# x multiplied by W1 ahead of the products of A, and 24 products of the last three rows made from fp32r halves

## The chip, the cores and the metric

The kernel runs on one core of a Trainium2 chip. The metric is the device time of one execution in microseconds (us); lower is better.

## What is computed

One layer over N = 8192 nodes with D = 128 features. `adj` is a dense 8192 x 8192 matrix of 268 MB, so reading it once is a large part of the time.

```
def _lap_mul(A, x):
    d = 1.0 / jnp.sqrt(jnp.sum(A, axis=-1))
    return d[:, None] * (A @ (d[:, None] * x))
z = _lap_mul(A, x) @ W1 + b1
z = jax.nn.leaky_relu(z, negative_slope=0.1)
sq = jnp.sum(z * z, axis=-1)
d2 = jnp.maximum(sq[:, None] + sq[None, :] - 2.0 * (z @ z.T), 0.0)
S = jnp.exp(-jnp.sqrt(d2 + 1e-10) / 2.0)
S = the 4 largest of each row of S, the rest zero
out = _lap_mul(S + A, x) @ W2 + b2
return _layernorm(x + out)
```

## The kernel before

A is cut into 16 x 16 tiles ("quads") of 512 rows by 512 columns. Tile (b, q) is row block b, column block q, and it arrives by one DMA of 1 MB into one of 18 slots in SBUF as 128 x 2048 numbers. Engines: PE is TensorE, DVE is VectorE, ACT is ScalarE, POOL is GpSimd, and SP issues the loads. Each engine runs its own list in the written order and waits on semaphores.

**Stage 1, rows 0 to 15.** For each row b, SP loads the 16 tiles of the row. DVE adds them one after the other into a running `total` (`add_quad`, line 1481), folds the total twice (`add_tiles`, 1486 and 1487), PE sums it over partitions (`row_sums`, 776), DVE copies the sums (`read_sums`, 1491), ACT takes the root (1046), DVE makes d by one Newton step (432 to 440) and scales x of that row by it (`scale_xs`, 1499). In between, PE multiplies tiles with those parts of the scaled x that already exist (`product`, 767): four fp32 matmuls of 128 x 512 for each tile. 158 of the 256 products are made in stage 1. A row's sum in PSUM is saved by ACT to R2 (1057) once its last product is made. A slot is loaded again after its tile was added and multiplied. At the end of row 15 the scaled x is split in two fp32r parts, a rounded one (ACT, 1031) and the rest (DVE, 1505).

**Stage 2.** The other 98 tiles are loaded again and multiplied from halves: ACT rounds the tile to fp32r (`round_2`, 1039), DVE subtracts to get the rest (`rest_2`, 1564), and PE makes eight matmuls with the rounded half (830 and 831) and four with the rest (834). Two buffers hold rounded halves, so the rounding of tile n waits for the product of tile n - 2. The rows of A come in the order 0, 15, 14, 1, 2, ..., 13. When a row is complete, its z is made beside the products of the next row: DVE adds the two parts of y (`make_y`, 1537), PE multiplies by W1 (`z_raw`, 796), DVE applies d, b1 and the leaky step (`make_z`, 1547 and 1550), PE transposes z back (`z_transposed`, 806), ACT squares (1070) and splits it (1076, 1079), DVE makes the rest (`make_zl`, 1556) and PE sums the squares (`squares`, 813). The table `made` says after which product each step stands.

**Stage 3 and later.** PE forms z z^T in pieces of 1024 columns (866 to 874), ACT copies them (1141), and DVE finds the largest of each row (1621, 1624), while A is read a third time for the last product, there with POOL making the rests (1299, 1442). The change leaves this part as it was, but for the steps at its start.

The order of the work is written out by hand, with counts at which a step is placed. Which slot a load goes to is worked out by `next_slot`, which takes the slot that comes free first.

Of the kernel before, what the change touches and what calls it, by code (L numbers as in the profile page):

```python
# [27 lines left out]
SLOTS_END = (0, 1, 2, 3, SLOTS_2, SLOTS_2 + B // TB)  # L28
# [7 lines left out]
LOW_AT = 10  # L36
ROW_BANKS = (2, 0, 3)
# [91 lines left out]
def build(nc, x, at, W1, b1, W2, b2, consts, out, xs_dram, xh_dram, xl_dram, acc_dram):  # L129
# [31 lines left out]
    for n in range(n_one + len(two)):  # L161
        if n < n_one - STREAM_END:
            k = next_slot(n, [*range(SLOTS_A), *(k for k, b in SLOTS_Y.items() if left(n) <= B * (b + 1)),
# [9 lines left out]
        now[k] = n  # L173
    last_in = {}
# [3 lines left out]
    with ctx:  # L178
# [25 lines left out]
        b1r = sb("b1r", [P, D])  # L204
# [19 lines left out]
        total = R1[:, N + 2 * SLOT:N + 3 * SLOT]  # L224
# [4 lines left out]
        y = tmp[:, 0:BC]  # L229
        zn = tmp[:, BC:2 * BC].rearrange("p (j d) -> p j d", j=TB)  # L230
        window = tmp[:, 2 * BC:2 * BC + WIN]
        junk = tmp[:, 2 * BC + 256:2 * BC + 256 + P]
# [34 lines left out]

        acc_x2 = sb("acc_x2", [P, len(ROWS_X) - 1, BC], at=top_of["xgl"])
# [6 lines left out]
        al_2 = [sb(f"al_2{k}", [P, TB, BC], F32R, at=top_of["R1"] + k * SLOT * 4) for k in range(2)]  # L275
        x_last = sb("x_last", [P, 2, 2, TB, D], F32R, at=over1 + 2 * SLOT * 4)
# [7 lines left out]
        spare = R2[:, (B - 1) * BC:B * BC]  # L284
        raw_t = [R1[:, k * SLOT:(k + 1) * SLOT].rearrange("p (k c) -> p k c", c=BC) for k in range(3)]
# [52 lines left out]
        xl_ok = sem("xl_ok")  # L338
        rnd_2 = sem("rnd_2")
        al_ok = sem("al_ok")  # L340
        y_ok = sem("y_ok")
        zraw = sem("zraw")
        zn_ok = sem("zn_ok")
        sq_ok = sem("sq_ok")
        zt = sem("zt")
# [99 lines left out]
        halves = range(min(q for r, q in two), B)  # L445
# [16 lines left out]
        for n, (b, q) in enumerate(two):  # L462
            last_quad[b] = n + 1
        CHAIN = 9
# [181 lines left out]
        def _(sp):  # L646
# [6 lines left out]
            sp.dma_start(b1r[:, :], b1.partition_broadcast(P)).then_inc(s_const, 16)  # L653
            sp.dma_start(b2r[:, :], b2.partition_broadcast(P)).then_inc(s_const, 16)
            for n, (b, q) in enumerate(one + two):
# [11 lines left out]
                if n < n_one and n % B == B // 2:  # L667
# [4 lines left out]
                    sp.dma_start(xs[:, tiles], x[:, tiles]).then_inc(s_x[n // B], 16)  # L672
# [81 lines left out]
        def _(pe):  # L754
# [3 lines left out]
            def product(b, q):  # L758
# [5 lines left out]
                if first and b >= YB:  # L764
                    pe.wait_ge(y_saved, b - YB + 1)
                for k in range(TB):
                    i = pe.matmul(PS[:, b % YB], xs[:, q * TB + k], slots_a[slot_of[n]][:, k],  # L767
                                  start=first and k == 0, stop=prod_at[b, q] == closed[b] and k == TB - 1)
                i.then_inc(prod1, 1)

            def row_sums(b):
                pe.wait_ge(part_ok, b + 1)
                if b >= 1:
                    pe.wait_ge(sums_read, b)
# [4 lines left out]
            for b in range(B):  # L779
                sums_at = len(products[b]) - (SUMS_EARLY if b == B - 1 else 0)  # L780
                for r, q in products[b][:sums_at]:
# [8 lines left out]
            def z_raw(pi):  # L790
                b = blocks2[pi]
                pe.wait_ge(y_ok, pi + 1)
                if pi >= 1:
                    pe.wait_ge(zn_ok, pi)
                for j in range(TB):
                    i = pe.matmul(PS[:, 4, j * P:(j + 1) * P], y[:, j * P:(j + 1) * P], w1[:, :],
                                  start=True, stop=True)
                i.then_inc(zraw, 1)

            def z_transposed(pi):  # L800
                pe.wait_ge(zn_ok, pi + 1)
                if pi >= 1:
                    pe.wait_ge(zl_ok, pi)
                    pe.wait_ge(z2_ok, pi)
                for j in range(TB):
                    i = pe.transpose(PS[:, 5, j * P:(j + 1) * P], zn[:, j], ident[:, :])
                i.then_inc(zt, 1)
# [11 lines left out]
            assert made[B - 2] == len(two) - 1  # L819
            for n, (b, q) in enumerate(two):  # L820
# [6 lines left out]
                pe.wait_ge(xl_ok, q - halves[0] + 1)  # L827
# [9 lines left out]
                for pi in range(B):  # L837
                    if n == made[pi] + 6:
                        squares(pi)
                    if n == made[pi] + 3:  # L840
                        z_transposed(pi)
                    if n == made[pi]:
                        z_raw(pi)


            def scores(g, j, c, first):
# [3 lines left out]
                if first and j == 0:  # L850
                    pe.wait_ge(z2_ok, min(B, 2 * c + 4))
# [73 lines left out]
            def group_pe(g, odd):  # L925
                for j in range(GT):
                    for c in range(NE):
                        scores(g, j, c, is_first(g))
                        if is_first(g) and (j, c) == (0, 0):
                            z_raw(B - 1)  # L930
                            z_transposed(B - 2)
                            squares(B - 3)
                        if is_first(g) and (j, c) == (0, 1):
                            z_transposed(B - 1)
                            squares(B - 2)
                        if is_first(g) and (j, c) == (0, 2):
                            squares(B - 1)
                        if is_first(g) and (j, c) == (PLAIN_TILES - 1, NE - 1):
# [834 lines left out]
```

## Time and profile before

| | us |
|---|---|
| median of 3 runs | 2691.74 (2691.24 to 2696.32) |
| span of the profiled execution, first to last instruction | 2759.5 |
| stage 1, to the end of its last product | 719.8 |
| stage 2, from there to the end of its last product | 306.4 |
| first score tile complete and everything after | the rest |

The profiled execution shows no time of its own beside its span; the first instruction stands 0.3 us after its start. The stages are read from the chain of work that ended last, whose rows carry start and duration.

### The profile page before, as it was taken

How to read it: one execution, taken by the hardware profiler on the slowest of the kernel's cores; microseconds unless marked ns; L12 is line 12 of the kernel's file. 1: busy time of each engine (PE TensorE's matmuls, PEld its weight loads, DVE VectorE, ACT ScalarE, POOL GpSimd, SP SyncE). 2: the span in 40 equal slices, each digit the busy share in tenths (PEclk: the TensorE clock that was granted, in tenths of full speed). 3: DMA queues.
4: the chain of work that ended last, by engine and by line, in shares of the span. 5: the costliest groups of instructions: out<-in, count | busy, mean ns of one | idle time of the engine just before them, and what ended most of it. 6: DMA issues, size and time to landing. Idle time of an engine off the chain costs nothing.

```text
span 2759.5 us, 29107 instructions
## 1 busy us (share of the span) xinstructions
PE 2482.6 (90%) x9356; PEld 1722.4 (62%) x9356; DVE 2319.8 (84%) x1411; ACT 1606.7 (58%) x1905; POOL 1195.4 (43%) x987
## 2 busy tenths in 40 slices
PE   1367999999999998899999999999999987888978
PEld 0133444444677776578787877778787764666655
DVE  7998899977788888999999999999999773666766
ACT  0000000000477767999989899899988763555655
POOL 0000000000000000377778878788878956666760
PEclk9688999999999999999999999999999988999989
DMA  9999999995899960146555655555655688988975
GB/s 385 421 402 408 398 421 421 421 421 215 320 349 342 338 226 7 35 141 183 151 163 138 179 142 175 140 170 149 174 143 167 182 309 343 347 324 320 345 295 208
DMA packets 147949, 718.58 MB, mean 260 GB/s; under 512 B 19025, under 2 KB 26961, under 8 KB 86609
## 3 DMA queue, kind: packets, MB, share of 16 engines
q1 hardware_dynamic: 124384, 670.49, 65.6%
q0 software_dynamic: 18800, 37.77, 5.7%
q10 hardware_dynamic: 4608, 8.39, 0.8%
q8 instruction: 79, 1.29, 0.2%
q14 instruction: 78, 0.63, 0.1%
HBM read 680.40 MB, written 36.18 MB: 260 GB/s over the span
## 4 chain that ended last, share of the span: by engine, by line
PE 56%; issue 10%; ACT 10%; DVE 9%; DMA 7%; POOL 3%; another core or an unknown queue 3%; SPq 0%; ACTq 0%; POOLq 0%; DVEq 0%
PE PS L767 17%; PE PS L866 5%; PE PS L868 5%; PE PS L867 5%; DMA ring<-at 4%; ACT R L1141 3%; PE PS L834 3%; PE PS L910 3%; PE PS L921 3%; PE PS L911 3%; PE PS L830 2%; PE PS L831 2%; ACT ah_t L1191 2%; DVE R L1621 2%
## 5 line engine op out<-in xcount | busy, mean ns | idle before, releaser
L1299 POOL TENSOR_TENSOR al<-ring,ah 128x1024 fp32r<-128x1024 f32 x264 | 644.0, 2441 | 180.5 <-ACT ah L1112 168.7
L1621 DVE MAX8 R<-R 128x8 f32<-128x8192 f32 x64 | 555.9, 8685 | 68.1 <-ACT R L1141 67.9
L1141 ACT ACTIVATE R<-PS 128x1024 f32<-128x1024 f32 x512 | 518.1, 1018 | 114.1 <-PE PS L874 83.1
L1624 DVE FIND_INDEX8 R<-R,R 128x8 uint32<-128x8192 f32 x64 | 555.9, 8685 | 0.3 <-issue 0.3
L1272 POOL CAST zst<-zh 128x128 fp32r<-128x128 f32 (+1 forms) x64 | 26.2, 410 | 1113.2 <-DVE zl L1556 811.5
L866 PE MATMUL PS<-zh,zst 128*128 128x512 f32 x1024 | 407.3, 398 | 28.6 <-ACT PS L1127 12.7
L868 PE MATMUL PS<-zh,zst 128*128 128x512 f32 x1024 | 400.4, 391 | 0.0
L867 PE MATMUL PS<-zl,zst 128*128 128x512 f32 x1024 | 400.1, 391 | 0.0
L1456 POOL DMA_INDIRECT R<-xs_dram,R x256 | 279.7, 1093 | 145.2 <-issue 75.5
L1127 ACT ACTIVATE PS<-R 128x1024 f32<-128x1024 f32 x310 | 318.0, 1026 | 6.6
L1046 ACT ACTIVATE tiny<-rowsum 128x4 f32<-128x4 f32 x16 | 3.3, 205 | 481.2 <-DVE rowsum L1491 481.2
L767 PE MATMUL PS<-cache,R 128*128 128x512 f32 x584 | 262.9, 602 | 17.0 <-DMA cache<-at 11.6
L1481 DVE TENSOR_TENSOR R<-R,cache 128x2048 f32<-128x2048 f32 x106 | 242.9, 2292 | 21.2 <-DMA cache<-at 19.0
L866 PEld LDWEIGHTS PS<-zh,zst 128*128 128x128 f32 x1024 | 192.1, 188 | 97.0 <-ACT PS L1127 25.3
L981 PE MATMUL PS<-ah_t,xsh 128*128 128x512 f32 x368 | 162.9, 443 | 63.9 <-ACT ah_t L1191 45.0
L868 PEld LDWEIGHTS PS<-zh,zst 128*128 128x128 f32 x1024 | 192.2, 188 | 41.7
L867 PEld LDWEIGHTS PS<-zl,zst 128*128 128x128 f32 x1024 | 192.3, 188 | 39.8 <-issue 0.7
L767 PEld LDWEIGHTS PS<-cache,R 128*128 128x128 f32 x584 | 112.1, 193 | 157.6 <-issue 144.1
L767 PE MATMUL PS<-ring,R 128*128 128x512 f32 x384 | 177.4, 610 | 11.2 <-DMA ring<-at 5.7
L1564 DVE TENSOR_TENSOR al<-ring,ah 128x2048 fp32r<-128x2048 f32 x66 | 151.0, 2290 | 35.6 <-ACT ah L1039 33.1
L1481 DVE TENSOR_TENSOR R<-R,ring 128x2048 f32<-128x2048 f32 x72 | 165.0, 2292 | 11.5 <-DMA ring<-at 9.6
L1668 DVE TENSOR_TENSOR al_t<-R,ah_t 128x1024 fp32r<-128x1024 f32 x98 | 115.7, 1221 | 63.2 <-ACT ah_t L1191 36.9
(177 smaller groups left out, 4469.9 us busy)
## 6 DMA issues: line engine op xcount, KB each, us to landing
R<-at SPq DMA_DIRECT2D x152, 1024.0 KB, 13.3
ring<-at SPq DMA_DIRECT2D x148, 1024.0 KB, 9.5
ring<-at SPq DMA_DIRECT2D x264, 512.0 KB, 3.9
cache<-at SPq DMA_DIRECT2D x117, 1024.0 KB, 20.2
raw_sq<-at SPq DMA_DIRECT2D x21, 1024.0 KB
raw_z<-at SPq DMA_DIRECT2D x20, 1024.0 KB
raw_ring<-at SPq DMA_DIRECT2D x20, 1024.0 KB
acc_dram<-R POOLq DMA_DIRECT2D x78, 256.0 KB, 5.7
```

The costliest lines, as they stand in the source:

```text
L767: i = pe.matmul(PS[:, b % YB], xs[:, q * TB + k], slots_a[slot_of[n]][:, k], start=first and k == 0, stop=prod_at[b, q] == closed[b] and k ...
L866: pe.matmul(bank, zst[:, par, 0], zh[:, cols], start=not on_seed, stop=False, skip_group_check=True)
L867: pe.matmul(bank, zst[:, par, 0], zl[:, cols], start=False, stop=False, skip_group_check=True)
L868: i = pe.matmul(bank, zst[:, par, 1], zh[:, cols], start=False, stop=on_seed, skip_group_check=True)
L981: pe.matmul(bank, xsh[:, t], ah_t[n % 2][:, k], start=from_zero and k == 0, stop=False, skip_group_check=True)
L1127: act.activation(pair(False, 0, c), sq_row[c], ACT.Copy).then_inc(seeded, 1)
L1141: act.activation(score[j % 2][:, c * EC:(c + 1) * EC].rearrange("p (b c) -> p b c", b=2), pair(first, j, c), ACT.Copy).then_inc(copied, 1)
L1299: pool.tensor_tensor(al[:, k % SPLIT], raw[k % RAW], ah[:, k % SPLIT].bitcast(F32), ALU.subtract)\
L1456: pool.indirect_dma_start(gx[f % 2][:, j, m], None, xs_dram, bass.IndirectOffsetOnAxis(ap=sidx[:, FIN[f] * TB + j, m:m + 1], axis=0))\
L1481: v.tensor_tensor(total.rearrange("p (k c) -> p k c", c=BC), other, slots_a[slot_of[n]], ALU.add)\
L1621: v.max(top[:, j], score[j % 2]).then_inc(dve3, 1)
L1624: v.max_index(place[:, j], top[:, j], score[j % 2]).then_inc(placed, 1)
```

## The change

W1 is moved ahead of A: since (A (d x)) W1 = A (d (x W1)), PE multiplies each x block by W1 in stage 1 (`x_w1`, from a transposed copy of x, `xt`, that is loaded in place of x), and ACT copies the product over x (`xw_ok`) before DVE scales it. In stage 2 the multiplication by W1 and the transposes of z are gone. In their place d lies along the free axis: PE transposes it once (`turn_d`), ACT writes it to DRAM, and ACT's queue loads it again for each row, spread over all partitions (`load_d`), so that DVE multiplies y by it; ACT adds b1 (`add_b1`). The squares come from one small transpose for each half of the rows (`turn_squares`, `read_squares`) in place of ACT's accumulating squares.

In rows 13, 14 and 15, the 8 products of each row with column blocks 0 to 7 are made from halves as in stage 2: ACT rounds the tile (`round_1`), POOL subtracts and writes the rest over the tile (`low_1`), PE makes 8 + 4 fp32r matmuls (`product_of_halves`). The halves of x for these blocks are made in row 12 (`high_of_low_q` on ACT, four subtractions on POOL). The order of the products of these rows is mixed (`mixed`). From row 12 on the running total lies in PSUM, and four of the slots are no longer loaded.

```
-STREAM_END = 12
+STREAM_END = 5
+LATE, TOTAL_AT, QL = 13, 12, 8
+W1_EARLY = 3
...
+            def x_w1(b):
+                pe.wait_ge(s_x[b], 16)
                 if b >= 1:
                     pe.wait_ge(sums_read, b)
                 for j in range(TB):
+                    i = pe.matmul(PS[:, YB, j * P:(j + 1) * P], xs[:, b * TB + j], w1[:, :], start=True, stop=True)
+                i.then_inc(xw, 1)
+
+            def product_of_halves(b, q, first):
+                m = half_1[b, q]
+                low = low_1[slot_of[load_at[b, q]]]
+                pe.wait_ge(xl_low_q, 4)
+                pe.wait_ge(rnd_1, m + 1)
+                for k in range(TB):
+                    t = q * TB + k
+                    pe.matmul(PS[:, y_bank(b)], xsh[:, t], ah_2[m % 2][:, k], start=first and k == 0, stop=False)
+                    pe.matmul(PS[:, y_bank(b)], xl_q[:, t], ah_2[m % 2][:, k], start=False, stop=False)
+                pe.wait_ge(al_1, m + 1)
+                for k in range(TB):
+                    i = pe.matmul(PS[:, y_bank(b)], xsh[:, q * TB + k], low[:, k], start=False, stop=False)
+                i.then_inc(prod1, 1)
...
-            def z_raw(pi):
...
-            def z_transposed(pi):
...
+            def round_1(m):
+                n = load_at[halved_1[m]]
+                act.wait_ge(ld_a[slot_of[n]], turn_of[n])
+                if m < 2:
+                    free_of_stage_1(act, SLOTS_B + m)
+                else:
+                    act.wait_ge(prod1, prod_at[halved_1[m - 2]])
+                act.activation(ah_2[m % 2][:, :, :], slots_a[slot_of[n]], ACT.Copy).then_inc(rnd_1, 1)
...
+            def add_b1(pi):
+                act.wait_ge(y_ok, pi + 1)
...
+                act.activation(z[pi % 2], y[pi % 2], ACT.Identity, bias=b1c[:, 0:1]).then_inc(biased, 1)
+                if pi + 2 < B:
+                    load_d(pi + 2)
...
+            for m, bq in enumerate(halved_1):
+                n = load_at[bq]
+                raw_1 = slots_a[slot_of[n]]
+                pool.wait_ge(rnd_1, m + 1)
+                pool.wait_ge(rows_added, (B - 1) * (n // B) + max(n % B, 1))
+                pool.tensor_tensor(low_1[slot_of[n]][:, :, :], raw_1, ah_2[m % 2][:, :, :].bitcast(F32), ALU.subtract)\
+                    .then_inc(al_1, 1)
...
+                running = PS[:, 3:3 + TB] if b >= TOTAL_AT else total
+                other = slots_a[slot_of[n - 1]] if i == 1 else running
+                v.tensor_tensor(total if i == B - 1 else running, other, slots_a[slot_of[n]], ALU.add)\
...
                     v.wait_ge(prod2, last_quad[b])
-                    v.tensor_tensor(y, cols, PS[:, bank_2[b]], ALU.add).then_inc(y_ok, 1)
+                    link(v.tensor_tensor(y[pi % 2], cols, PS[:, bank_2[b]], ALU.add))
+                    cols = y[pi % 2]
+                v.wait_ge(s_d_all[pi % 2], 16 * (pi // 2 + 1))
+                v.tensor_tensor(y[pi % 2], cols, d_all[:, pi % 2], ALU.mult).then_inc(y_ok, 1)
```

PE at the turn from row 12 to row 13. Before, the sums of row 12 (L776) stand among products that are all fp32 (cache, ring, R_49 and R_50 on the left of the comma are slots of tiles; a count stands for matmuls of 128 x 512):

```order
L767 MATMUL PS<-R_50,R_49 128x512 x4
L767 MATMUL PS<-cache,R_49 128x512 x12
L776 MATMUL PS<-ones,R_49 128x1 x4
L767 MATMUL PS<-ring,R_49 128x512 x4
L767 MATMUL PS<-R_49 128x512 x4
L767 MATMUL PS<-cache,R_49 128x512 x20
```

In the changed kernel the same place has x W1 of row 12 (L835) three products ahead of the sums (L856), and after two whole products the first one from halves (rounded halves ah, rests low; the pair L845, L846 stands four times):

```order
L835 MATMUL PS<-w_58,R_49 128x128 x4
L826 MATMUL PS<-cache,R_49 128x512 x8
L826 MATMUL PS<-ring,R_49 128x512 x4
L856 MATMUL PS<-ones,R_49 128x1 x4
L826 MATMUL PS<-cache,R_49 128x512 x4
L826 MATMUL PS<-ring,R_49 128x512 x4
L845 MATMUL PS<-ah_83,xsh 128x512
L846 MATMUL PS<-ah_83,xl_q 128x512
...
L849 MATMUL PS<-low_90,xsh 128x512 x4
```

Four 128 x 128 matmuls came in ahead of each row's sums, and a halved product now stands where a whole one did.

DVE in stage 2, from the eighth y of the stage on (al is the rest of a tile). Before:

```order
L1537 TENSOR_TENSOR R_49<-R_50,PS 128x512
L1564 TENSOR_TENSOR al_83<-R_49,ah_81 128x2048
L1564 TENSOR_TENSOR al_84<-R_49,ah_82 128x2048
L1547 SCALAR_TENSOR_TENSOR R_49<-PS,dsc,b1r 128x128 x4
L1550 SCALAR_TENSOR_TENSOR R_49<-R_49 128x512
L1564 TENSOR_TENSOR al_83<-ring,ah_81 128x2048
```

and the same place in the changed kernel:

```order
L1701 TENSOR_TENSOR R_49<-R_50,PS 128x512
L1704 TENSOR_TENSOR R_49<-R_49,d_all 128x512
L1723 TENSOR_TENSOR al_85<-R_49,ah_83 128x2048
L1723 TENSOR_TENSOR al_86<-R_49,ah_84 128x2048
L1708 SCALAR_TENSOR_TENSOR R_49<-R_49 128x512
```

The four small steps are gone from the second gap between rests, and a second step of 512 columns has come into the first one.

ACT in stage 2, beside the steps of one row's z (ah is the rounded half). Before:

```order
L1039 ACTIVATE ah_82<-ring 128x2048
L1070 ACTIVATE R_49,sq<-R_49 128x128 x4
L1039 ACTIVATE ah_81<-R_49 128x2048
L1076 ACTIVATE zh<-PS 128x512
L1079 ACTIVATE R_49<-PS 128x512
```

And in the changed kernel:

```order
L1118 ACTIVATE ah_83<-R_49 128x2048
L1212 ACTIVATE yz_odd<-yz_odd,b1c 128x512
L1205 DMA d_all<-d_dram 128x512
L1118 ACTIVATE ah_84<-R_49 128x2048
L1118 ACTIVATE ah_83<-ring 128x2048
L1219 ACTIVATE zh<-yz_odd 128x512
L1222 ACTIVATE R_49<-yz_odd 128x512
```

The four squares are replaced by one step of 512 columns and a DMA that ACT issues.

## Rows read from the trace of the kernel before

**Rows 1.** The head of the page.

```profile
span 2759.5 us, 29107 instructions
```

**Rows 2.** Chain that ended last, stages 1 and 2: start, duration, what.

```profile
268.30 40.42 PE PS L767 x88
...
607.60 51.61 PE PS L767 x120
...
709.39 10.41 PE PS L767 x24
...
1024.94 1.21 PE PS L834 x4
```

**Rows 3.** Timeline of PE at the sums of row 14: start, duration, instructions.

```profile
659.04 0.95 PE L776 MATMUL PS<-ones,R 128*128 128x1 f32 x8
659.85 3.68 PE L767 MATMUL PS<-cache,R 128*128 128x512 f32 x8
```

**Rows 4.** Timeline of PE in rows 4 to 6; idle time before, and its releaser.

```profile
218.83 1.87 PE L776 MATMUL PS<-ones,R 128*128 128x1 f32 x8 [5.50 <-DVE R L1487]
...
268.30 6.09 PE L767 MATMUL PS<-ring,R 128*128 128x512 f32 x8 [3.81 <-DMA ring<-at]
```

**Rows 5.** Busy time by stretch: length, engines' busy us, clock, DMA share, GB/s.

```profile
621.00:690.00 69.00, 69.00 (x169) 30.97 (x168) 48.83 (x31) 6.07 (x12) 0.00 (x0) 1.00 0.57 216
```

**Rows 6.** Groups of instructions, later stages: count, busy us, mean ns, idle before.

```profile
L1442 POOL TENSOR_TENSOR al_t<-R,ah_t 128x2048 fp32r<-128x2048 f32 x2 | 9.1, 4558 | 0.5 <-ACT ah_t L1191 0.5
L1299 POOL TENSOR_TENSOR al<-ring,ah 128x1024 fp32r<-128x1024 f32 x264 | 644.0, 2441 | 180.5 <-ACT ah L1112 168.7 <-PE PS L921 1.6 <-POOL d2s L1354 0.6
...
L1624 DVE FIND_INDEX8 R<-R,R 128x8 uint32<-128x8192 f32 x64 | 555.9, 8685 | 0.3 <-issue 0.3
```

**Rows 7.** Groups of instructions up to 1100 us.

```profile
L1481 DVE TENSOR_TENSOR R<-R,cache 128x2048 f32<-128x2048 f32 x106 | 242.9, 2292 | 21.2 <-DMA cache<-at 19.0
...
L1057 ACT ACTIVATE R<-PS 128x512 f32<-128x512 f32 x16 | 9.1, 596 | 215.1 <-PE PS L767 215.1
```

**Rows 8.** Timeline of PE over one row of stage 2.

```profile
843.46 0.39 PE L830 MATMUL PS<-ah,xsh 128*128 128x512 f32 x1
...
846.18 0.39 PE L830 MATMUL PS<-ah,xsh 128*128 128x512 f32 x1
...
849.05 1.05 PE L796 MATMUL PS<-w,R 128*128 128x128 f32 x8
849.86 0.47 PE L830 MATMUL PS<-ah,xsh 128*128 128x512 f32 x1
...
851.79 1.08 PE L834 MATMUL PS<-al,xsh 128*128 128x512 f32 x4
...
858.60 0.60 PE L806 MATMUL PS<-ident,R 128*128 128x128 f32 x4
858.95 0.48 PE L830 MATMUL PS<-ah,xsh 128*128 128x512 f32 x1
...
867.40 1.02 PE L813 MATMUL PS<-R 128*128 128x512 f32 x2
867.85 0.79 PE L830 MATMUL PS<-ah,xsh 128*128 128x512 f32 x1
...
873.74 1.05 PE L796 MATMUL PS<-w,R 128*128 128x128 f32 x8
```

**Rows 9.** Timeline of DVE over the same row of stage 2.

```profile
851.25 2.29 DVE L1564 TENSOR_TENSOR al<-R,ah 128x2048 fp32r<-128x2048 f32 x1 [0.49 <-ACT ah L1039]
...
854.62 0.69 DVE L1550 SCALAR_TENSOR_TENSOR R<-R 128x512 f32<-128x512 f32 x1
```

**Rows 10.** Timeline of ACT over the same row of stage 2.

```profile
852.96 1.92 ACT L1039 ACTIVATE ah<-ring 128x2048 fp32r<-128x2048 f32 x1 [1.74 <-PE PS L834]
```

**Rows 11.** Timeline of PE at the sixth and seventh score piece.

```profile
1042.18 0.39 PE L866 MATMUL PS<-zh,zst 128*128 128x512 f32 x1
...
1043.99 0.39 PE L866 MATMUL PS<-zh,zst 128*128 128x512 f32 x1
```

More of the change, by code:

```diff
@@ L83, in held, with mixed, y_bank, row_of_y_bank @@
     return range(b - DEFER[b], b)
+def mixed(b):
+    plain, halved = list(range(QL, b)), list(range(QL))
+    order = [plain.pop(0), plain.pop(0)]
+    n_plain, n_halved, taken = len(plain), len(halved), 0
+    while plain or halved:
+        if halved and (QL - len(halved) + 1) * n_plain <= (taken + 1) * n_halved or not plain:
+            order.append(halved.pop(0))
+        else:
+            order.append(plain.pop(0))
+            taken += 1
+    return order
+def y_bank(b):
+    return b % YB if b < 9 else (b + 2) % 3
+def row_of_y_bank(b):
+    return b - YB if b < 12 and b != 10 and b != 11 else b - 3
 def plan_ab():
@@ L173, in build @@
         now[k] = n
+    order_1 = []
+    for b in range(B):
+        sums_at = len(products[b]) - (SUMS_EARLY if b == B - 1 else 0)
+        order_1 += [(b, q) for b, q in products[b][:sums_at]] + [("sums", b)] + products[b][sums_at:]
+    order_1 += products[B]
+    place_1 = {what: n for n, what in enumerate(order_1)}
+    halved_1 = [(b, q) for b, q in flat if b >= LATE and q < QL]
+    half_1 = {bq: m for m, bq in enumerate(halved_1)}
+    last_whole = max(prod_at[bq] for bq in flat if bq[1] < QL and bq not in half_1)
     last_in = {}
@@ L444, in build @@
         ends = list(itertools.accumulate(sum(r == b for r, q in two) for b in blocks2))
-        halves = range(min(q for r, q in two), B)
+        halves = range(QL, B)
         last_quad = {}
@@ new lines, in after @@
+            def after(k):
+                return place_1[one[last_in[k]]] + 0.5
+            steps = []
+            for b in range(TOTAL_AT, B):
+                steps.append((place_1["sums", b] + 0.7, "root", b))
+            for b in range(saved, B):
+                steps.append((place_1[flat[closed[b] - 1]] + 0.6, "save", b))
+            for k in range(2):
+                steps.append((after(SLOTS_2 + k), "high", k))
+            steps.append((after(SLOTS_2 + B // TB + 1), "move", 0))
+            for q in halves[:-2]:
+                steps.append((max(after(SLOTS_2 + k // TB) for k in range(QL, q + 1)) + 2.2 + q / 100, "half", q))
@@ new lines, in _ @@
+            for m in range(len(halved_1)):
+                at_m = place_1[halved_1[m - 2]] + 0.5 if m >= 2 else place_1[halved_1[m]] - 3.5
+                steps.append((at_m, "round", m))
+            for _, what, k in sorted(steps):
+                if what == "root":
+                    b = k
+                    act.wait_ge(xw, b + 1)
+                    act.activation(xs[:, b * TB:(b + 1) * TB], PS[:, YB].rearrange("p (j d) -> p j d", j=TB), ACT.Copy)\
+                       .then_inc(xw_ok, 1)
+                    root_of_row(b)
+                    if b == B - 1:
+                        round_2(0)
+                        for q in halves[-2:]:
+                            high_half(q)
+                        round_2(1)
+                if what == "save":
+                    save_y(k)
+                if what == "high":
+                    high_of_low_q(k)
+                if what == "move":
+                    move_low()
+                if what == "half":
+                    high_half(k)
+                if what == "round":
+                    round_1(k)
```

267 lines of the change are left out of this document (157 added, 110 removed).

## The prediction

> **What bounds the kernel now.** I read the page first for the span [rows 1], then the chain that ended last, then PE's timeline where the chain is PE, and last the timelines of DVE and ACT in stage 2. The profiled execution spans 2759.5 us; the median of the runs is 2691.74, 67.8 lower. I make the sum in the profiled execution's microseconds and take the difference over to the median as it is: the stretches that change are PE's own work, one matmul behind the other, and no row tells which stretch the 67.8 lie in.
>
> The chain shows that from 268.30 on stage 1 is PE alone: 40 to 52 us of line 767 at a time, broken only by the row sums, to 719.8 [rows 2]. 120 records are 15 products, so a product costs 51.61 / 15 = 3.44 us; the sums cost 0.81 (659.04 to 659.85) [rows 3]. Up to 268 PE waits for others: 5.50 us for DVE's total at row 4's sums, 3.81 for a load at row 6's first product [rows 4]. In the last rows the DMA is only 57% busy while PE is busy throughout [rows 5], so PE time saved there needs no faster loads.
>
> Stage 2 (719.8 to 1026.15, 306.4 us) is also a dense PE, but a tight one. A product from halves takes 2.72 (843.46 to 846.18) [rows 8]. Round 2 of tile n starts only after product n - 2: ACT 1.92, DVE 2.29, and the rest must be there when PE has done the first two thirds of product n. With about 0.26 from product to ACT (the start at 852.96 [rows 10]; the four matmuls from 851.79 take 0.91 [rows 8]) and 0.1 for the two handovers, that is 0.26 + 1.92 + 2.29 + 0.1 = 4.57, against 2.72 + 1.81 = 4.53 on PE. So anything put between two rests on DVE that is longer than its gap (0.49 before the rest at 851.25 [rows 9]) is a wait on PE.
>
> **The change part by part.**
>
> *x W1 in stage 1 costs 8.7.* The same four matmuls as z_raw: 849.05 to 849.86 and 0.08 on the first record after (0.47 against 0.39), 0.89 [rows 8]; the row sums, also eight records, cost 0.81. I take 0.87. In rows 0 to 5 PE waits for longer than that [rows 4], so it is hidden; if that cover fails it is 5 more. In rows 6 to 15 it is on the path: 10 x 0.87 = 8.7. ACT's copy of it has three products (10 us) to finish 0.6 us of work [rows 7].
>
> *24 products from halves give 17.2.* 24 x (3.44 - 2.72).
>
> *Their supply takes back 5.* POOL's subtraction of 128 x 2048 is 4.56 us [rows 6], twice DVE's. 24 of them are 109 us, and PE spends about 147 us on these three rows (row 13: 8 x 2.72 + 6 x 3.44 + 1.7 = 44), so POOL keeps up on average. Locally it doesn't: with two buffers, product m can't end before product m - 2 plus 0.26 + 1.92 + 4.56 + 0.05 + 0.91 = 7.7, where two halved products in a row need 5.44. A third in a row waits 2.3. The order has three in a row twice, both in row 13: (13,2) to (13,4), and (13,5) to (13,7), where the queue on POOL is partly made up by then: 2.3 + 1.4. Pairs wait 0.2 to 0.6, five of them: 1.3. Bounds: 0, were the rounds early enough, and 17, where nothing is gained.
>
> *DVE and POOL in the same rows: 7, unknown.* POOL's first subtraction of a row starts when DVE has added that tile, the third load of the row; DVE then does the Newton steps and scale_xs from SBUF and after them the add that frees POOL's next subtraction. If these DVE steps had to wait while POOL reads SBUF, each of rows 13 and 14 loses 4.56 less 0.5 of slack on its second halved product; row 15, with a whole product between, 1.5; and add_tiles of row 15 comes up to two subtractions late, of which 3.4 reach PE. Sum 13. The other end is 0: in the later stages DVE's FIND_INDEX8, listed with two inputs from SBUF, takes 8685 ns beside POOL's 2441 [rows 6], both undisturbed. But its second input is eight values, so that row doesn't decide; I take the middle, 7. The Trainium skill ("SBUF — State Buffer", Who interferes with whom) says that a DVE instruction with two SBUF inputs and a GpSimd one that reads SBUF exclude each other for a whole instruction; by it this term is 13 and the sum 6 worse. No row before has such a pair. With the total in PSUM the 14 later adds of a row have one SBUF input and stay clear of it.
>
> *Loads.* From row 12 on there are four slots less. A load then goes into a slot whose product is about 10 places (30 us) back, against 4.9 us for 1 MB at the 216 GB/s of these rows [rows 5]: 0. The last load waits for (15,4), leaving three products (8.9) for the load (4.9), its add (2.29) and a fold of about 2: 0.3, inside the 5.
>
> *Stage 2 gives 12.* Gone for each row: z_raw 0.89 and the transposes 0.43 (0.35 and 0.08) [rows 8], 15 and 14 times before the end: 19.4. Squares stay at 0.86. One row of 8 products now takes 24.69 (849.05 to 873.74): 21.76 + 0.89 + 0.43 + 0.86 leave 0.75 of waits. In the changed order DVE has the add and the multiplication by d in one gap: 0.6 + 0.04 + 0.6 (a 128 x 512 step counts 0.69 [rows 9], of which I take 0.6 for one in a stream), 1.24 less 0.43 is 0.8 of wait; add_b1 waits for it and delays the next rounding, another 0.3. So 1.1 a row against 0.75. By these prices the 98 products, 14 squares and 1.1 x 14 make 266.6 + 12 + 15.4 = 294, 12.4 less than 306.4. Bounds: no waits, -27; twice the waits, +3. turn_d, turn_squares, the copy of d and ACT's wait for the write of d at the fifth product: 1 to 4 us once; 2.
>
> *The start of the scores gives 2.5.* Before, the sixth piece starts at 1042.18 [rows 11], 16.0 after stage 2. A piece takes 1.81 (1042.18 to 1043.99). After: five pieces (9.1), three squares of 0.86 (2.6), and by estimate 1.8 for turn_squares, a first wait and the copy of the squares: 13.5. ACT's squares and PE's two transposes were on that path. Bounds 0 and -4.
>
> Sum: 8.7 - 17.2 + 5 + 7 - 12.4 + 2 - 2.5 = -9.4. Later stages stay. **Forecast 2682.3 us.**
>
> **The rivals.**
>
> *No exclusion between DVE and POOL* (0 in place of 7): -16.4, 2675. For it: nothing in the trace shows the two disturb each other. Against: no such pair stands in it.
>
> *Full exclusion* (the rule above): -3.4, 2688. Its sign would be lost in the measurement, 0.2% or 5.4 us.
>
> *POOL sets the pace, and the kernel is slower.* 4.56 is from two instructions beside other DVE work. At more than 5.2 us most subtractions (some 17 of 24) end after PE wants them, and each further 0.1 us costs 1.7. With the -9.4 it decides from about 5.6; at 6.0 it gives +11, 2703. Against: 264 subtractions of half the size agree at 2441.
>
> *Stage 2 gives nothing.* DVE's step is late because d lands late (each load_d of 256 KB runs beside a DMA near its full rate) or the waits are 2 us a row: the 12.4 go, +3, 2695. Against: load_d is issued two rows ahead, 14 us or more.
>
> **How the numbers follow.** Chances: forecast (that term between 3 and 10) 0.40, no exclusion 0.18, full exclusion 0.20, POOL paced 0.12, stage 2 nothing 0.10. The forecast's own range is 2676 to 2688. For 8 in 10 the range must take in full and no exclusion with the bounds of stage 2's waits, and part of the slower cases: 2669 to 2699. Faster: 0.36 of the forecast's 0.40, the 0.18 and 0.06 of full exclusion, 0.60. Slower: the 0.12 and 0.03 of the last, 0.15. Same: 0.25.
>
> **What would show it.** In rows 6 to 12 the sums should lie 0.87 further apart. In rows 13 to 15 the whole products stay at 3.44 and halved ones stand at 2.72 with waits for POOL near (13,4) and (13,7); if DVE's short Newton steps stand some 4 us apart there, exclusion is real. A subtraction on POOL over 5 us speaks for the third rival. Stage 2 should last 296 and its row of 8 products 23.7 to 23.8, with PE waiting for the rest once after each y. The sixth score piece should start about 13.5 after the last product. I am wrong if stage 1 ends later than 727 or stage 2 lasts over 302.

## The result

The changed kernel takes 2703.07 us (median of 6 runs, 2698.41 to 2704.70), the kernel before 2692.23 (6 runs); the ratio is 1.0032, 95% interval 1.0022 to 1.0043. It is 10.8 us or 0.3% slower, where 9.4 us less were forecast, and the time lies outside the forecast's range of 2669 to 2699.

The head of the changed kernel's page, then PE's timeline at some row sums (L856), at the last product of stage 1 (L826) and at the last one of stage 2 (L913): start, duration, what, and in brackets the idle time before and its releaser.

```profile
span 2701.3 us, 29187 instructions
```

```profile
350.19 0.95 PE L856 MATMUL PS<-ones,R 128*128 128x1 f32 x8
...
393.17 0.95 PE L856 MATMUL PS<-ones,R 128*128 128x1 f32 x8
...
561.68 0.95 PE L856 MATMUL PS<-ones,R 128*128 128x1 f32 x8
...
724.81 1.85 PE L856 MATMUL PS<-ones,R 128*128 128x1 f32 x8 [3.26 <-DVE R L1655]
...
735.18 3.60 PE L826 MATMUL PS<-ring,R 128*128 128x512 f32 x8
...
1036.79 1.19 PE L913 MATMUL PS<-al,x_last 128*128 128x512 f32 x4
```

DVE's timeline at the first search for the largest scores:

```profile
1059.28 8.68 DVE L1792 MAX8 R<-R 128x8 f32<-128x8192 f32 x1
```

The same two places in the kernel before, the sums of row 12 (PE) and the first search (DVE):

```profile
557.69 0.95 PE L776 MATMUL PS<-ones,R 128*128 128x1 f32 x8
```

```profile
1048.99 8.70 DVE L1621 MAX8 R<-R 128x8 f32<-128x8192 f32 x1 [7.56 <-ACT R L1141]
```

Before, the sums of row 12 stood at 557.69, stage 1 ended at 719.8, stage 2 at 1026.15 [rows 2], and the first MAX8 at 1048.99. Now they are at 561.68, 738.6 (735.18 + 3.44), 1038.0 and 1059.28. So up to row 12 the change costs 4.0; rows 13 to 15 take 176.9 where they took 162.1, +14.8; stage 2 takes 299.4 where it took 306.4, -7.0; the start of the scores takes 21.3 where it took 22.8, -1.5. That is +10.3 at the first MAX8, which is the whole loss within the spread of the runs.

The loss is made in rows 13 to 15. PE's timeline at four halved products and the products behind them (L849 are the matmuls with the rest, L826 whole products):

```profile
577.90 1.93 PE L849 MATMUL PS<-low,xsh 128*128 128x512 f32 x4 [3.72 <-POOL low L1429]
579.64 4.52 PE L826 MATMUL PS<-cache,R 128*128 128x512 f32 x8
...
597.06 1.20 PE L849 MATMUL PS<-low,xsh 128*128 128x512 f32 x4 [2.19 <-POOL low L1429]
598.09 5.29 PE L826 MATMUL PS<-ring,R 128*128 128x512 f32 x8
...
614.25 1.20 PE L849 MATMUL PS<-low,xsh 128*128 128x512 f32 x4 [2.67 <-POOL low L1429]
615.29 5.29 PE L826 MATMUL PS<-cache,R 128*128 128x512 f32 x8
...
636.62 2.07 PE L849 MATMUL PS<-low,xsh 128*128 128x512 f32 x4 [3.72 <-POOL low L1429]
```

Each time PE waits for the rest, and the whole product behind the wait takes 4.1 to 5.3 (4.11 behind the last, at 638.50) in place of 3.60 as listed. The group of these matmuls up to 1060 us (busy, mean ns, idle before) shows the sum of such waits, 14.4:

```profile
L849 PE MATMUL PS<-low,xsh 128*128 128x512 f32 x96 | 29.0, 427 | 14.4 <-POOL low L1429 14.4
```

Why the rest is late stands in the timelines of POOL (first fence) and DVE (second) at the start of row 13:

```profile
565.19 4.51 POOL L1429 TENSOR_TENSOR low<-ring,ah 128x2048 fp32r<-128x2048 f32 x1 [7.17 <-DVE PS L1649]
573.32 13.71 POOL L1429 TENSOR_TENSOR low<-cache,ah 128x2048 fp32r<-128x2048 f32 x3 [3.61 <-DVE PS L1649]
```

```profile
565.16 0.16 DVE L487 TENSOR_TENSOR tiny<-tiny 128x4 f32<-128x4 f32 x1
565.36 4.37 DVE L488 TENSOR_TENSOR tiny<-tiny,rowsum 128x4 f32<-128x4 f32 x1
569.87 0.17 DVE L490 TENSOR_SCALAR tiny<-tiny 128x4 f32<-128x4 f32 x1
...
719.06 4.97 DVE L1654 TENSOR_TENSOR R<-R 128x1024 f32<-128x1024 f32 x1
```

A Newton step on 128 x 4 numbers takes 4.37 and ends at 569.73, when POOL's subtraction ends (569.70). The add that POOL's second subtraction needs stands behind it on DVE, so POOL idles 3.61 and PE waits 3.72. The same repeats in row 14 (624.09). At the end of row 15 the fold (L1654, 1.2 to 1.4 in the rows before) takes 4.97 beside a subtraction, and PE waits 3.26 before the last sums.

What the waits leave behind is in the busy times by stretch (length, PE, PEld, DVE, ACT, POOL, granted clock, DMA share, GB/s):

```profile
572.00:580.00 8.00, 4.28 (x15) 3.17 (x14) 7.90 (x4) 1.98 (x2) 6.55 (x2) 0.88 0.66 266
580.00:598.00 18.00, 15.81 (x52) 9.71 (x51) 17.73 (x9) 6.28 (x4) 12.60 (x4) 0.96 0.69 263
598.00:603.00 5.00, 5.00 (x11) 2.16 (x9) 4.90 (x4) 1.91 (x1) 5.00 (x2) 0.66 0.83 318
...
615.00:621.00 6.00, 6.00 (x16) 2.89 (x16) 0.00 (x0) 2.39 (x2) 0.00 (x0) 0.72 1.01 427
621.00:638.50 17.50, 13.78 (x45) 8.41 (x45) 16.71 (x12) 2.12 (x2) 10.83 (x3) 0.93 0.73 263
638.50:661.00 22.50, 21.92 (x73) 13.67 (x72) 22.16 (x11) 8.25 (x5) 17.38 (x5) 0.98 0.75 296
...
718.00:726.50 8.50, 5.24 (x22) 3.95 (x21) 8.43 (x7) 3.00 (x6) 4.95 (x2) 0.90 0.69 247
726.50:732.00 5.50, 5.50 (x14) 4.32 (x15) 4.37 (x13) 3.05 (x4) 0.00 (x0) 0.53 0.00 0
```

From 598 to 603 PE is busy throughout at a mean of 0.66 of the full clock, for at least 2 us of it, 599 to 601, at 0.50, the lower of its two levels (1.2 of 2.4 GHz); before this it had waited 2.19. Length times missing share over these eight rows is 10.2 us, a little of it idle. In the kernel before, the clock was 1.00 in the stretch of these rows that is shown [rows 5], and it is 1.00 over all of them (557.69 to 719.80).

Stage 2: DVE (first fence) and PE (second) around one y.

```profile
864.54 0.68 DVE L1701 TENSOR_TENSOR yz_odd<-R,PS 128x512 f32<-128x512 f32 x1
865.25 0.69 DVE L1704 TENSOR_TENSOR yz_odd<-yz_odd,d_all 128x512 f32<-128x512 f32 x1
865.86 2.28 DVE L1723 TENSOR_TENSOR al<-R,ah 128x2048 fp32r<-128x2048 f32 x1
```

```profile
868.20 1.19 PE L913 MATMUL PS<-al,xsh 128*128 128x512 f32 x4 [0.52 <-DVE al L1723]
...
892.23 1.20 PE L913 MATMUL PS<-al,xsh 128*128 128x512 f32 x4 [0.45 <-DVE al L1723]
```

A row of eight products is 24.03 long (868.20 to 892.23), where it was 24.69 [rows 8].

### The profile page after: what moved, and what is told of

Read it like the earlier page. It is cut to its first block, busy times and chain, and to the rows that moved or that the text cites. A ratio compares the mean times of both kernels' runs of the same rounds, so it can differ in the third digit from the quotient of the medians.

```text
span 2701.3 us, 29187 instructions
## 1 busy us (share of the span) xinstructions
PE 2459.1 (91%) x9405; PEld 1729.9 (64%) x9405; DVE 2346.9 (87%) x1363; ACT 1655.7 (61%) x1835; POOL 1320.0 (49%) x1015
## 4 chain that ended last, share of the span: by engine, by line
PE 51%; ACT 14%; DVE 11%; issue 11%; DMA 9%; POOL 4%; SPq 0%; ACTq 0%; POOLq 0%; DVEq 0%
PE PS L826 14%; ACT R L1293 6%; DMA ring<-at 5%; PE PS L945 4%; PE PS L947 4%; PE PS L946 4%; PE PS L1049 3%; PE PS L989 2%; PE PS L1000 2%; PE PS L990 2%; PE PS L913 2%; ACT PS L1278 2%; DMA raw_sq<-at 2%; DVE R L1792 2%; DVE al_t L1839 2%
## 5 line engine op out<-in xcount | busy, mean ns | idle before, releaser
L945 PE MATMUL PS<-zh,zst 128*128 128x512 f32 x1024 | 408.4, 399 | 29.4 <-ACT PS L1278 12.4
L1422 POOL TENSOR_TENSOR xl_q<-R,xsh 128x1024 fp32r<-128x1024 f32 x4 | 10.7, 2708 | 546.9 <-PE PS L826 546.9
L826 PE MATMUL PS<-cache,R 128*128 128x512 f32 x496 | 225.0, 604 | 5.7 <-DVE R L1667 5.7
L1649 DVE TENSOR_TENSOR R<-R,cache 128x2048 f32<-128x2048 f32 x78 | 178.8, 2292 | 13.8 <-DMA cache<-at 12.4
L1059 PE MATMUL PS<-ah_t,xsh 128*128 128x512 f32 x368 | 155.4, 422 | 19.1 <-ACT ah_t L1342 19.0
L826 PEld LDWEIGHTS PS<-cache,R 128*128 128x128 f32 x496 | 95.6, 195 | 118.8 <-issue 117.7
L826 PE MATMUL PS<-ring,R 128*128 128x512 f32 x336 | 157.0, 614 | 7.9 <-DVE R L1667 5.4
L1263 ACT ACTIVATE ah<-ring 128x1024 fp32r<-128x1024 f32 x152 | 159.8, 1051 | 4.1 <-DMA ring<-at 4.1
L1118 ACT ACTIVATE ah<-ring 128x2048 fp32r<-128x2048 f32 x66 | 126.4, 1915 | 46.4 <-PE PS L913 43.5
```

Source lines behind the costliest of these rows:

```text
L826: i = pe.matmul(PS[:, y_bank(b)], xs[:, q * TB + k], slots_a[slot_of[n]][:, k], start=first and k == 0, stop=prod_at[b, q] == closed[b] an ...
L945: pe.matmul(bank, zst[:, par, 0], zh[:, cols], start=not on_seed, stop=False, skip_group_check=True)
L1263: act.activation(ah[:, k % SPLIT], raw[k % RAW], ACT.Copy).then_inc(rounded, 1)
L1649: v.tensor_tensor(total if i == B - 1 else running, other, slots_a[slot_of[n]], ALU.add)\
```

## The experiments

Rows 13 to 15 are counted from the sums of row 12 to the end of the last product of stage 1, since the loads shift the place of these sums by up to 4 us from run to run. Each kernel and the kernel before were timed on one chip, and the ratio is between these two; the chips differ from kernel to kernel, and the median of the kernel before lies between 2692.2 and 2695.0 on them. Stages are read from one profile each: split_y leaves rows 13 to 15 as they are in the changed kernel and shows 2.4 us less there, so differences of that size between two profiles say nothing.

| kernel | median us | ratio, interval | rows 13 to 15 | stage 2 |
|---|---|---|---|---|
| before (profile shown first) | 2692.23 | 1 | 162.1 | 306.4 |
| changed | 2703.07 | 1.0032 (1.0022 to 1.0043) | 176.9 | 299.4 |
| before_again, one run | 2694.47 | | 162.8 | 306.1 |
| w1_alone | 2691.13 | 0.9985 (0.9976 to 0.9994) | 164.2 | 298.1 |
| total_sbuf, one run | 2752.74 | | 228.2 | 299.7 |
| newton_psum | 2688.00 | 0.9979 (0.9970 to 0.9989) | 163.7 | 298.8 |
| fold_psum | 2696.59 | 1.0014 (1.0005 to 1.0023) | 168.4 | 298.6 |
| order | 2688.46 | 0.9977 (0.9969 to 0.9986) | 161.3 | 298.8 |
| split_y | 2699.55 | 1.0017 (1.0009 to 1.0026) | 174.5 | 295.2 |
| all4 | 2684.40 | 0.9963 (0.9950 to 0.9976) | 161.7 | 295.2 |
| all6 | 2671.07 | 0.9916 (0.9902 to 0.9929) | 149.5 | 295.0 |
| w1_split | 2684.78 | 0.9965 (0.9953 to 0.9977) | 164.2 | 294.2 |
| no_psum | 2673.24 | 0.9923 (0.9909 to 0.9936) | 150.9 | 295.7 |

### before_again: the kernel before, profiled once more

> The kernel before, unchanged, for a second profile: the one shown spans 2759.5 us, 67.8 above the median of its runs. If these 67.8 lie in the later stages, the span is near 2690 here, while stage 1 still ends at about 719.8, stage 2 still lasts about 306.4 and the first MAX8 still starts at about 1049. If they lie in stages 1 and 2, these stages are up to 67 us shorter here, and the comparison of stages between before and after falls.

Its page's head, and DVE's timeline at the first MAX8:

```profile
span 2692.6 us, 29107 instructions
```

```profile
1049.36 8.70 DVE L1621 MAX8 R<-R 128x8 f32<-128x8192 f32 x1 [7.56 <-ACT R L1141]
```

The first MAX8 is where it was (1049.36 and 1048.99), the span is 66.9 shorter. So the 67.8 between [rows 1] and the median lay in the later stages of that one execution, and the stages of before can be compared as they stand.

### w1_alone: only the W1 part

```
-STREAM_END = 5
-LATE, TOTAL_AT, QL = 13, 12, 8
+STREAM_END = 12
+LATE, TOTAL_AT, QL = B, B, 5
...
-            pool.wait_ge(prod1, last_whole)
...
```

> The changed kernel with the W1 part alone: no halves in rows 13 to 15, the total and the last loads of stage 1 as in the kernel before. Theory (the loss comes from the halves alone): sums lie 0.89 further apart as in the changed kernel, stage 1 ends at 719.8 + 4.0 (already there at the sums of row 12) + 3 x 0.89 = 726.5, stage 2 lasts 299.4 as in the changed kernel, the scores start 1.5 earlier; in all -1.8, 2690 us, ratio 0.9993. Rival (the W1 part loses): 2697 or more, with stage 1 ending after 733 or stage 2 lasting as long as before.

2691.13: the W1 part gains 3 us (ratio 0.9985). Rows 13 to 15 take 164.2, which is 162.1 and 3 x 0.89 less 0.6. So the halves cost 12.7 in rows 13 to 15 of the changed kernel (176.9 and 164.2), 11.9 by the medians as they stand and 14.0 by each kernel's difference to the kernel before on its chip, where bare durations (each product at its own length, no waits, full clock) give 17.2 back.

### total_sbuf and newton_psum: do DVE and POOL exclude each other?

The first leaves the running total in SBUF; the second lets each Newton step and the scaling read one of its two inputs from PSUM.

```
-                running = PS[:, 3:3 + TB] if b >= TOTAL_AT else total
+                running = total
```

```
+                    y0_ps, a_ps, d = (PS[:, YB, k * 2 * TB:k * 2 * TB + TB] for k in range(1, 4))
...
+                    link(v.reciprocal(y0_ps, root))
+                    link(v.tensor_tensor(a_ps, y0, y0_ps, ALU.mult))
+                    link(v.tensor_tensor(a, a_ps, rowsum[:, cols], ALU.mult))
...
-                v.tensor_tensor(xs[:, cols], xs[:, cols], bcast(dsc[:, cols], D), ALU.mult).then_inc(xs_ok, 1)
+                v.tensor_tensor(xs[:, cols], xs[:, cols], bcast(d, D), ALU.mult).then_inc(xs_ok, 1)
```

> The changed kernel with one edit: the running total of rows 12 to 15 stays in SBUF, so that every add of a tile has two SBUF inputs. Theory (such a DVE step and a POOL subtraction don't run at once): the adds (45 x 2.29 = 103 us in rows 13 to 15) and the 24 subtractions (109 us) must share 212 us, where sums of row 12 to the end of stage 1 now take 177; stage 1 ends some 30 us or more later, 2733 or more, with adds and subtractions in turn in the timelines. Rival (no exclusion of this kind): adds of 2.3 and subtractions of 4.6 side by side, 2703.

> The changed kernel, with the short Newton steps and the scaling of x in rows 12 on rewritten so that none of them reads two inputs from SBUF (one of the two lies in PSUM; two small steps more). Theory (a DVE step with two SBUF inputs and a POOL subtraction don't run at once): the 4.37 us step falls below 0.3 at its three places, the second subtraction of rows 13 and 14 starts some 4 us earlier, PE's waits of 3.72 there go to under 0.5, and the time lost at the lower clock behind them goes too: 8 to 10 us less than the changed kernel, 2693 to 2695. Rival (POOL is too slow for this order of products, wherever DVE's inputs lie): the 4.37 us step may stay or go, but PE's waits stay, 2703.

With the total in SBUF, the groups of adds (L1649) and subtractions (L1429) from 540 to 800 us:

```profile
L1649 DVE TENSOR_TENSOR R<-R,cache 128x2048 f32<-128x2048 f32 x25 | 105.6, 4224 | 0.7
...
L1429 POOL TENSOR_TENSOR low<-cache,ah 128x2048 fp32r<-128x2048 f32 x14 | 89.9, 6429 | 35.8 <-DVE R L1649 35.8
```

An add that takes 2.29 alone has a mean of 4.22, a subtraction of 4.5 one of 6.43. Where two meet, single adds last 6.5 (6.50 at 597.88) and single subtractions 6.6 (6.59 at 604.52), not far from the 6.8 of both together: they take turns. Rows 13 to 15 take 228.2, 51 more than in the changed kernel, whose total lies in PSUM from row 12 on: with one input there, its adds of 2.30 run beside the subtractions. In newton_psum, DVE at the same place of row 13 (first fence), POOL (second) and PE (third):

```profile
568.79 0.16 DVE L1674 TENSOR_TENSOR tiny<-PS,rowsum 128x4 f32<-128x4 f32 x1
```

```profile
568.41 4.53 POOL L1429 TENSOR_TENSOR low<-ring,ah 128x2048 fp32r<-128x2048 f32 x1 [7.16 <-DVE PS L1649]
572.89 13.87 POOL L1429 TENSOR_TENSOR low<-cache,ah 128x2048 fp32r<-128x2048 f32 x3
```

```profile
577.59 1.20 PE L849 MATMUL PS<-low,xsh 128*128 128x512 f32 x4 [0.19 <-POOL low L1429]
578.62 3.60 PE L826 MATMUL PS<-cache,R 128*128 128x512 f32 x8
```

The step takes 0.16 in the middle of the subtraction, the second subtraction follows without a gap, PE waits 0.19 in place of 3.72, and the whole product behind is back at 3.60. Rows 13 to 15 are 13.2 shorter: PE's waits there fall by 8.2 (7.1 of it at these two places) and its busy time, the same matmuls, by 5.0. That is more than the 8 to 10 that were expected, and the median, 2688.00, lies below 2693 to 2695. The theory holds and POOL's pace as the only cause falls; the waits at three halved products in a row stay (2.18 and 2.97).

### fold_psum: the fold with one input in PSUM

```
+                    v.tensor_tensor(total[:, 0:2], PS[:, 3:5], slots_a[slot_of[n]][:, 0:2], ALU.add)
+                    v.tensor_tensor(PS[:, 5:7], PS[:, 5:7], slots_a[slot_of[n]][:, 2:4], ALU.add).then_inc(rows_added, 1)
...
+                    link(v.tensor_tensor(half[:, 0:BC], total[:, 0], PS[:, 5], ALU.add))
+                    link(v.tensor_tensor(PS[:, 6], total[:, 1], PS[:, 6], ALU.add))
+                    v.tensor_tensor(part, half[:, 0:BC], PS[:, 6], ALU.add).then_inc(part_ok, 1)
```

> The changed kernel with the end of each total in rows 12 to 15 rewritten: the last add and the fold take one of their two inputs from PSUM (five steps of the same total length in place of three). Theory (a DVE step with two SBUF inputs and a POOL subtraction don't run at once): the fold of row 15, 4.97 us in the changed kernel, needs 1.2, its sums come at about 721.5 in place of 724.8, PE's wait of 3.26 there goes, and with it the half-speed products behind it: 5 to 7 us; the stretched subtractions of row 13 (5.56 and 5.96) shrink to 4.6, 1 to 2 us more. 2695 to 2698. Rival (row 15 waits for its late last loads, whatever the fold does): the fold may be shorter, but the sums stay at 724 to 725, 2702 or more.

DVE at the end of row 15:

```profile
720.38 0.69 DVE L1661 TENSOR_TENSOR R<-R,PS 128x512 f32<-128x512 f32 x1
...
722.43 5.46 DVE L1684 TENSOR_TENSOR xsl<-R,xsh 128x512 fp32r<-128x512 f32 x6
```

The fold is not held, PE's wait before the last sums is gone, and rows 13 to 15 are 8.5 shorter. The steps behind it, the low halves of x, have two SBUF inputs and are held in its place (5.46 for six steps that took 3.69). The two long subtractions of row 13 were expected to shrink to 4.6: one does (4.64), the other lasts 6.12 beside the first add of row 14, which reads two tiles in SBUF.

### order: no three halved products in a row

```
+ORDER_OF = {13: (8, 0, 9, 1, 2, 10, 3, 4, 11, 5, 6, 12, 7), 14: (8, 0, 9, 1, 2, 10, 3, 11, 4, 5, 12, 6, 13, 7), 15: (8, 0, 9, 1, 10, 2, 11, 3, 12, 4, 13, 5, 6, 7, 14)}
...
 def mixed(b):
-    plain, halved = list(range(QL, b)), list(range(QL))
...
+    return list(ORDER_OF[b])
```

> The changed kernel with another order of the products in rows 13 to 15: the first halved product stands second in its row, and no three halved ones follow each other in rows 13 and 14. Supply theory (two buffers and subtractions of 4.5 us don't feed three halved products in a row): the waits of 2.19 and 2.67 in row 13 fall to 0.6 or less, and with the slow products behind them this gives 6 to 8 us. The first subtraction of a row can then run ahead of the Newton steps, so that the 4.37 us step may go as well, up to 10 us more. 2688 to 2697. Rival (only the exclusion of DVE and POOL makes the waits): as long as Newton's step is 4.37, 2701 or more.

2688.46. PE has no wait for POOL in rows 13 and 14, and Newton's step takes 0.16, since POOL's first subtraction now ends before it. A new wait stands at the sums of row 13, and the same one, 2.64, at those of row 14:

```profile
612.57 1.52 PE L850 MATMUL PS<-ones,R 128*128 128x1 f32 x8 [2.64 <-ACT R L1177]
```

The sums wait for ACT's copy of x W1, which stands on ACT behind a rounding that waits for the row's last halved product. This edit removes both kinds of wait in these two rows at once, so alone it does not part supply from exclusion.

### split_y: multiplication by d in another gap of DVE

```
-                    if n == made[pi]:
-                        make_y(pi)
...
+                    if n == made[pi]:
+                        make_y(pi, not late)
+                    if late and n == made[pi] + 1:
+                        scale_y(pi, y[pi % 2] if b < B - 1 else R2[:, b * BC:(b + 1) * BC])
```

> The changed kernel with the multiplication of y by d moved behind the next rest, and the steps after it by one product each; the last three rows as they were. Theory (in stage 2 PE waits because DVE has two steps of 0.69 in one gap of 0.49): the product after each y takes 3.0 in place of 3.4 to 3.5, and add_b1 no longer waits; a row of eight products 23.4 to 23.6 in place of 24.03, stage 2 about 293 to 295 in place of 299.4, 2697 to 2699. Rival (stage 2 waits for ACT or for d's load, wherever DVE's step stands): stage 2 stays at 298 or more, 2702.

PE over one row of eight products:

```profile
877.68 1.20 PE L913 MATMUL PS<-al,x_last 128*128 128x512 f32 x4
...
901.33 1.21 PE L913 MATMUL PS<-al,x_last 128*128 128x512 f32 x4
```

23.65, where the changed kernel takes 24.03 (868.20 to 892.23). So the second step of y, in a gap of its own, costs PE less than behind the first. Stage 2 is 4.2 shorter (294.2 to 295.7 in the five kernels with this edit, 298.1 to 299.7 in the six with x W1 and without it), and all three figures fall just short of what was expected: 23.65 against 23.4 to 23.6, 295.2 against 293 to 295, 2699.55 against 2697 to 2699.

### all4 and all6

all4 has the four edits newton_psum, fold_psum, order and split_y. all6 has two more: ACT's copy of x W1 placed ahead of the next rounding, and the low halves of x behind the last Newton step.

```
                 steps.append((place_1["sums", b] + 0.7, "root", b))
+                steps.append((place_1["sums", b] - 4 + 0.55, "copy", b))
...
+            read_sums(B - 1)
+            scale_xs(B - 1)
             for q in halves[:-2]:
                 low_half(q)
-            read_sums(B - 1)
-            scale_xs(B - 1)
```

> The changed kernel with all four edits: Newton steps and fold with one input in PSUM, the other order of products, the multiplication by d moved. The excess of 27 us of rows 13 to 15 over the bare products goes but for 3 to 6, and stage 2 is 5 us shorter: 2674 to 2682, ratio to the kernel before 0.992 to 0.996. Rival (the edits cover the same waits, Newton's alone gave most of it): no better than that edit alone with the 5 of stage 2, 2684 or more.

> The kernel with four edits and two more: ACT copies the product x W1 ahead of the next rounding instead of behind it (in the four-edit kernel PE's sums of rows 13 and 14 wait 2.64 for that copy, with slow products behind), and DVE makes the low halves of x after the Newton step of row 15 (there they stand 7.78 us ahead of it, behind POOL's last subtraction, and PE waits 1.59). Theory: the excess of rows 12 to 15 over the bare products falls from 12.75 to 1 to 3, the end of stage 1 from 726.2 to about 715, 2671 to 2677. Rival (the waits only move to the next subtraction, since POOL is the bound of these rows): stage 1 ends at 722 or later, 2680 or more.

all4 missed its range (2684.40, where its rival said 2684 or more): its four edits take the old waits away, and new ones stand there. The sums of rows 13 and 14 wait 2.64 each, as in order. At the end of row 15, DVE (first fence), POOL (second) and PE (third):

```profile
712.23 7.78 DVE L1691 TENSOR_TENSOR xsl<-R,xsh 128x512 fp32r<-128x512 f32 x6
```

```profile
711.88 4.57 POOL L1424 TENSOR_TENSOR low<-ring,ah 128x2048 fp32r<-128x2048 f32 x1 [2.47 <-ACT ah L1145]
```

```profile
722.74 3.67 PE L820 MATMUL PS<-ring,R 128*128 128x512 f32 x8 [1.59 <-DVE R L1685]
```

With these two places mended, PE has one wait left in rows 13 to 15:

```profile
705.01 1.20 PE L843 MATMUL PS<-low,xsh 128*128 128x512 f32 x4 [1.20 <-POOL low L1427]
...
709.48 3.60 PE L820 MATMUL PS<-ring,R 128*128 128x512 f32 x8
```

Rows 13 to 15 take 149.5, and the kernel 2671.07, ratio 0.9916 to the kernel before: it is faster than the kernel before and the changed one.

### w1_split and no_psum

w1_split is w1_alone with split_y. no_psum is all6 without newton_psum and fold_psum.

> The W1 part alone with the multiplication of y by d moved: no halves in rows 13 to 15. It is the one before which the worth of the halves is read. From the W1 part alone (2691.1) and the move (4 in the changed kernel): 2687, ratio 0.997. If the halves are worth their 24 x 0.72 = 17 us once they are supplied, the six-edit kernel is 14 to 17 below this one; if POOL bounds these rows whatever the order, 8 or less.

> The six-edit kernel without the two edits that put an input in PSUM: Newton steps and fold read two inputs from SBUF as in the changed kernel; order of products, copy of x W1, low halves and the multiplication by d as in the six-edit kernel. Theory (the exclusion costs only where a step meets a subtraction in time): with the other order the Newton steps of rows 13 and 14 meet none (0.16 in the order edit alone), only a fold and the subtraction beside it are stretched by some 4 us off PE's path; 2671 to 2675. Rival (two SBUF inputs on DVE cost in rows 13 to 15 wherever they stand): 2680 or more.

Without halves rows 13 to 15 take 164.2, with halves well supplied 149.5: they give 14.7 of the bare 17.2 there, and 13.7 in the medians. And with the other order the PSUM edits are worth little: rows 13 to 15 of no_psum take 1.4 more than in all6, and the intervals of the two ratios overlap (2673.24 and 2671.07). In row 14 of it DVE is still held, at a Newton step and at the fold:

```profile
611.90 2.13 DVE L481 TENSOR_TENSOR tiny<-tiny 128x4 f32<-128x4 f32 x1
...
649.90 4.95 DVE L1653 TENSOR_TENSOR R<-R 128x512 f32<-128x512 f32 x1
```

but PE waits only once more than in all6, 1.53 in row 14.

## Why the prediction was wrong

*x W1 in stage 1.* Right: the sums of rows 7 and 8 are 42.98 apart (350.19 to 393.17), which is 12 x 3.435 + 0.81 + 0.89 = 42.92. In this profile it costs 6.7, not 8.7: 4.0 up to row 12 and 3 x 0.89, since PE's wait for a load before row 6 [rows 4] is shorter there. In the other runs with x W1 the sums of row 12 stand up to 3.8 later, so 8.7 is not shown wrong.

*24 products from halves.* Right: 2.72 each, and 14.7 of the 17.2 are got in all6.

*Supply (5) and exclusion (7).* The step that failed first: the exclusion term. I took the middle of 0 and 13, with only the row of FIND_INDEX8 [rows 6] for 0, which didn't decide. The exclusion is full: total_sbuf and newton_psum show it from both sides, and the prediction's sign for it, Newton steps 4 us apart, is in the trace. PE's waits in rows 13 to 15 are 14.4 for POOL and 3.26 before the last sums, 17.7; by the prediction's own bound full exclusion gives 5 + 13 = 18. Stage 1 so ends at 738.6, later than the 727 that I named as a sign of being wrong. The Trainium skill's rule ("SBUF — State Buffer", Who interferes with whom) is what the trace shows: a DVE step with two SBUF inputs and POOL's subtraction take turns for whole instructions (4.37 for a step of 0.16), and with one input in PSUM they don't (0.16).

*The step that was missing: PE after a wait.* I priced a wait at its own length and the products behind it at nothing more. PE in rows 13 to 15 of the changed kernel (first) and of all6 (second), in the columns of the busy times above:

```profile
561.68:738.60 176.92, 159.29 (x521) 98.53 (x520) 151.28 (x88) 55.42 (x43) 112.81 (x24) 0.94 0.73 277
```

```profile
563.43:712.90 149.47, 148.27 (x521) 93.34 (x520) 127.37 (x102) 55.48 (x43) 108.43 (x24) 1.00 0.83 321
```

The same 521 matmul records are busy for 159.29 at a mean clock of 0.94, and for 148.27 at 1.00 where the waits are gone: 11.0. Over the runs the clock of these rows falls with the waits: 1.00 in the kernels without halves, 0.97 with 9.4 of waits (newton_psum), 0.87 with 54 (total_sbuf). The other way round, of the 29.3 that rows 13 to 15 lose (14.8 more than before, where bare durations give 14.5 less), 17.7 are waits, and 11.6 are left, of which the windows' clock explains about 10.2. This carries the sum from a small gain to a loss: full exclusion's -3.4 and 11.6 make +8.2; with 3.4 and 1.0 more for the stage-2 and score terms below and 2.0 less for x W1 it is +10.6, against +10.3 in the profile.

*POOL paced, the third rival.* No, and that its 2703 is the measured time is luck: undisturbed subtractions take 4.5 to 4.6, not 6.0, and the price was added up wrongly. By its own 1.7 for each 0.1 us above 5.2, a subtraction of 6.0 gives 13.6 - 9.4 = +4, 2696, and not +11. The few that last over 5 us stand beside a DVE step with two SBUF inputs, so the sign that I named for this rival was a sign of exclusion. Its place, three halved products in a row, is real: waits of 2.19 and 2.67 there, where I expected 2.3 and 1.4, and order removes them. The second holds some 1.5 of exclusion that I had overlooked: the subtraction it waits for lasts 5.96 (608.24), since it starts beside the first add of the next row, which reads two tiles in SBUF and ends at 609.79.

*Loads.* 0 holds: all6 has the same slots, and its rows 13 to 15 take 149.5 where I counted about 147 of PE's work.

*Stage 2.* -7.0, not -10.4 (-12.4 and +2). The mechanism is right: one wait at each y, from two DVE steps in one gap; split_y takes 4.2 of it back. The row of eight is 24.03 in place of 23.7 to 23.8, and the stage has some 3 more than I priced; how they divide is open.

*Start of the scores.* -1.5, not -2.5.

How far fold_psum, newton_psum and order cover the same waits is open: alone they shorten rows 13 to 15 by 8.5, 13.2 and 15.6, 37.3 together, where all6 gains 27.4 with all edits. That they do overlap is plain: no_psum has the order without the other two and comes within 1.4 of all6.

## What to carry to other kernels

Work moved to a free engine is not free if its operands meet a neighbour's in SBUF: look for every two-input step of DVE that can fall beside a POOL instruction, the small ones too, since a step of 0.16 holds up what is queued behind it for the length of a POOL instruction. There are two ways out, each shown by one edit alone: one input in PSUM (newton_psum), or an order in which the step meets no POOL instruction (order). The second has to be looked at again after every other edit: in no_psum a Newton step is held again. A wait on a dense PE is to be priced with the slow products behind it; here 17.7 us of waits brought 11.6 more. And when one wait is removed, look at what was queued behind it on each engine: two of the six edits mend waits that stood out only with the other four.

## What the runs showed of the hardware

A step that reads the same tile twice counts as one with two SBUF inputs: a product of tiny with itself took 2.13 beside a subtraction (no_psum) and 0.16 elsewhere. After a wait of only 2.19 on PE the granted clock of the next 5 us is 0.66, in a row that runs at 1.00 in the kernel before. Two profiles of the kernel before, 67 us apart in span, are 0.4 us apart at the first MAX8.
